# Two shifted copies inside SBUF: ScalarE's own copies against DMAs that ScalarE issues

## The reference

```python
pooled = x.mean(axis=(-2, -1))
gate = jax.nn.softmax(pooled @ gate_w.T + gate_b)
kw1 = jnp.einsum('be,eoihw->boihw', gate, experts_w1) + conv1_w      # kw2, kb1, kb2 likewise
out1 = jax.nn.relu(per_sample(x, kw1, kb1))                            # 3x3, SAME
out2 = per_sample(out1, kw2, kb2)                                      # 3x3, SAME
return identity + out2 * RES_SCALE
...
x = x + _L0_conv_ref(_gn(x), ...)
```

## Time and profile before

| | |
|---|---|
| median of 3 runs | 386.82 us (386.42, 386.82, 389.31) |
| span of the profiled execution | 389.2 us, first to last instruction |
| the profiled execution's own time | 389.31 us, the one of the three that holds the span |
| busy: PE, DVE, ACT, POOL | 84%, 79%, 77%, 11% of the span |
| mean granted TensorE clock | 0.940 of full speed |
| DMA traffic | 58.19 MB, mean 149 GB/s |

### The profile page before, as it was taken

The page is one execution under the profiler, slowest core; times in us unless marked ns, Lnnn a source line. Parts: engine busy times, 40 slices in busy tenths (PEclk is TensorE's granted clock), DMA queues, the critical chain, the costliest instruction groups (busy, mean ns, idle before and its releaser), DMA issues.

```text
span 389.2 us, 8418 instructions
## 1 busy us (share of the span) xinstructions
PE 326.8 (84%) x2983; PEld 198.4 (51%) x2983; DVE 308.1 (79%) x709; ACT 300.3 (77%) x373; POOL 44.5 (11%) x80
## 2 busy tenths in 40 slices
PE   3218698996999699996979979996999979999984
PEld 2117345654555355653535555653656545655663
DVE  4899978988689886998688797898689897777432
ACT  2357499986897968977897868978789768976950
POOL 7262302010100101010000101010010101000000
PEclk9556999998999989998999989999999989999998
DMA  7949915495948959396856949497885956092354
GB/s 169 224 95 196 205 30 125 107 203 137 202 92 187 182 142 220 86 210 148 178 127 149 223 111 203 96 196 147 188 167 123 217 128 147 22 207 53 92 123 121
DMA packets 107146, 58.19 MB, mean 149 GB/s; under 512 B 102496, under 2 KB 103008, under 8 KB 107104
## 3 DMA queue, kind: packets, MB, share of 16 engines
q1 hardware_dynamic: 106912, 57.62, 69.7%
q0 software_dynamic: 192, 0.01, 0.1%
HBM read 19.47 MB, written 18.87 MB: 99 GB/s over the span
## 4 chain that ended last, share of the span: by engine, by line
DVE 39%; PE 22%; issue 15%; ACT 13%; DMA 6%; SPq 3%; DVEq 1%; ACTq 0%
PE pg L393 20%; DVE mix L677 11%; DVE a L706 6%; DVE stats L621 6%; DVE img L718 5%; DMA c<-a 5%; ACT c L558 4%; ACT a L544 4%; ACT hid L544 2%; DVE a L668 2%; DVE wts L696 2%; DVE wts L699 2%; SPq L282 1%; DVE gate L661 1%; PE pg L357 1%
## 5 line engine op out<-in xcount | busy, mean ns | idle before, releaser
L393 PE MATMUL pg<-a,wts 128*64 128x480 f16 (+1 forms) x1440 | 303.5, 368 | 24.8 <-DVE img L718 18.2
L393 PE MATMUL pg<-c,wts 128*64 128x480 f16 (+1 forms) x1440 | 308.3, 372 | 6.1 <-ACT a L544 3.2
L393 PEld LDWEIGHTS pg<-c,wts 128*64 128x64 f16 x1440 | 156.1, 111 | 81.7 <-issue 6.8
L393 PEld LDWEIGHTS pg<-a,wts 128*64 128x64 f16 x1440 | 156.1, 112 | 64.5 <-issue 14.6
L544 ACT ACTIVATE hid<-pg,col 128x480 f32<-128x480 f32 (+3 forms) x112 | 58.9, 541 | 47.6 <-PE pg L393 25.6
L558 ACT COPY c<-a 64x2352 f32<-64x2352 f32 x32 | 68.7, 2148 | 0.2
L677 DVE SCALAR_TENSOR_TENSOR mix<-bank,gate,mix 128x386 f32<-128x386 f32 x96 | 63.9, 665 | 2.3
L706 DVE TENSOR_TENSOR a<-hid,a 128x480 f16<-128x480 f32 (+3 forms) x112 | 54.9, 512 | 12.2 <-ACT a L544 11.6
L544 ACT ACTIVATE a<-pg,col 128x480 f16<-128x480 f32 (+3 forms) x112 | 59.2, 544 | 0.4
L718 DVE SCALAR_TENSOR_TENSOR img<-pg,img 128x480 f32<-128x480 f32 (+1 forms) x80 | 48.1, 631 | 11.2 <-PE pg L393 9.9
L621 DVE BATCH_NORM_STATS2 stats<-img 128x6 f32<-128x384 f32 x96 | 45.5, 541 | 0.0
(11 more groups left out here) (60 smaller groups left out, 133.8 us busy)
## 6 DMA issues: line engine op xcount, KB each, us to landing
c<-a SPq DMA_DIRECT2D x28, 588.0 KB, 9.0
img<-in_x SPq DMA_DIRECT2D x56, 288.0 KB, 5.3
out<-img SPq DMA_DIRECT2D x60, 180.0 KB, 2.9
out<-img SPq DMA_DIRECT2D x60, 108.0 KB, 1.9
c<-a SPq DMA_DIRECT2D x8, 294.0 KB, 4.4
img<-in_x SPq DMA_DIRECT2D x16, 144.0 KB, 4.4
out<-img SPq DMA_DIRECT2D x4, 120.0 KB, 2.1
out<-img SPq DMA_DIRECT2D x8, 60.0 KB, 1.7
```

The lines of the kernel that those rows point to most:

```text
L393: last = nc.tensor.matmul(pg[g][side * 64:side * 64 + 64, at:at + nb * W].rearrange("p (b w) -> p b w", w=W), wts[s.c % WSETS][kind][:, v, ...
```

## The change

The two copies by ScalarE's datapath (L558, each of 64 partitions, seen as 32-bit words to halve their number) become two DMAs that ScalarE issues in the same place of its program. The waits ahead of them are the same. The DMAs read the same rows of `a2`, shifted by one block in one of the two halves, and write `c2`. TensorE's wait changes from one count by ScalarE to the landing of both DMAs (16 each), and the semaphore is split over a ring of six, so that the counts of two images are not mixed.

```diff
-        crossed2 = sem("crossed2")
+        crossed2 = [sem(f"crossed2_{i}") for i in range(RING)]
...
-                    pe.wait_ge(crossed2, s.number + 1)
+                    pe.wait_ge(crossed2[s.ring], 32 * (s.lap + 1))
...
-                d, a = (halves(k[t.parity])[half].rearrange("p a b w -> p a (b w)").bitcast(F32) for k in (c2, a2))
-                first = (1 - half) * RP // 2
-                last = nc.scalar.copy(d, a[:, :, first:first + NB * RP // 2])
-                if half == 1:
-                    last.then_inc(crossed2, 1)
+                first = 1 - half
+                act.dma_start(halves(c2[t.parity])[half][:, :, :, :].rearrange("p a b w -> p a (b w)"),
+                              halves(a2[t.parity])[half][:, :, first:first + NB, :].rearrange("p a b w -> p a (b w)")
+                              ).then_inc(crossed2[t.ring], 16)
```

## The result

The change costs 12%: **435.03 us** (4 runs, 432.43 to 437.19) against 387.23 (4 runs, 386.42 to 389.31), a ratio of 1.1203 with a 95% interval of 1.1132 to 1.1273. The forecast of 446 had the direction, the range and the size right, 59 us for a measured 48. Two of its reasons were not right, and the experiments show what stands in their place.

What follows compares the result with a forecast made beforehand. No engine has much room, so event order decides: PE would wait at conv2, 25.7 us a slot. Slots 2 to 15 add 52, slot 1 adds 5, slot 16 adds 2: 59 on 386.8 gives 446 us, range 408 to 492.

Steps and rivals of the forecast that it cites:

- The rhythm of before and its margin: Kernel before: 21.98 us a slot; `c2` ready 0.7 us early, 5.0 us from start of making to use.
- The size of the stall: PE at conv2 in each slot: waits for `c2` by L less 5.0, so 5.0 us.
- L: ScalarE's DMA pair for `c2`: time from first issue's start to the second DMA's landing, taken as 10.0 us.
- Slot 1: First slot's wait for `c2`: L about 9 in place of 4.3 us, costing 5 us.
- The clock: PE behind the stall at conv2: lower granted clock costs another 1.6 us a slot.
- The gap at the start of a slot goes away: PE ahead of conv1: no wait remains, since finish of group 0 is long done and VectorE has slack.
- the sharing of the engines: Two queues sharing DMA engines evenly: cross2's 6.0 us of transfer stretched by another 6.0, upper L 14.2.
- SP's stores start earlier and give time back to cross1: SP's queue: earlier stores give back some 3 us, so cross1 lands about 25.7 us into the slot, not 28.7.
- The DMA engines as the bound: Rival for every slot: L 14.2, slot 29.9 us, total 507, or 488 with cross1 as gate; chance 0.16.
- The faster side: Rival: pair lands within 5.0 us, PE doesn't wait, VectorE's lag sets the slot; 361 to 374 us, chance 0.04.
- ScalarE's freed time: Copies leaving ScalarE: 2.2 to 3.1 us a slot stay free, gain counted as nothing if PE waits at conv2.

Runs made afterwards that it cites:

- The filler: Changed kernel plus five unneeded fp32 matmuls ahead of TensorE's wait for `c2` in every slot: 443.58 us, runs from 427.52 to 449.63.
- the reorder: Changed kernel with cross1 issued ahead of the loads in SP's order from slot 2 on: 414.41 us, 1.060; the same edit in the kernel before: 0.991.
- the kernel with idle DMAs: Kernel before, keeping ScalarE's copies, plus the change's two DMAs in the same place into a tile that nobody reads: 427.22 us, ratio 1.094.
- the twelfth-size kernel: Changed kernel with each `c2` DMA moving 2 of 24 block rows, the rest of `c2` set to zero once: 377.16 us, ratio 0.967.

## Why the prediction was right, and where its steps were not

**The rhythm of before and its margin** held: 5.0 us from start to use, cross1 as the gate of every other slot. PE waits for `c2` in each slot, as forecast.

**The size of the stall** was off, 5.0 us forecast and 2.7 in most slots. L was taken as 10.0 and is 8.7 in slot 4: that is 1.3 us. ScalarE issues 1.1 us ahead of the place where its copies began, which I had as a bound only: that is the rest. In slots 3 and 11, where the pair took 11.7 and 11.4 us, the stall was over 5.

**Slot 1** was to cost 5 us and cost 1.5. L is 9.3 there, as forecast (about 9), but the pair goes out at 52.15, 3.2 us ahead of the copies of before (55.38 in the earlier trace rows).

**The clock** was as forecast, 1.7 us, in 11 of the 13 slots from 2 to 14. The length of the wait alone does not decide it: over the four microseconds behind a wait of 2.38 us in slot 13 the granted clock is 0.66, behind 1.89 us in slot 10 and 2.41 us in slot 14 it is 1.00, and so it is behind 3.44 us in slot 4 of the changed kernel with cross1 first. The filler shows that its cost is partly hidden behind cross1.

**"The gap at the start of a slot goes away"** failed ahead of three slots, with 2.4 to 2.8 us each. Two of these gaps are cross1's; the third, 2.42 us ahead of slot 8, ends on nothing that the profile names. Ahead of six others cross1 landed 0.6 us or less before PE began. The step that failed is the sharing of the engines: I stretched cross2 by the other queue's traffic, up to 14.2. In most slots it is SP's issues that are stretched, the loads' by 5 us in slot 4, and cross2 comes through almost undisturbed. That SP's stores start earlier and give time back to cross1 was right: they start 2.3 us ahead of slot 4, where they started 2.3 us into slot 10 before. So the two changes nearly cancel: cross1 lands 23.6 us into the slot, where 25.7 was forecast and 22.7 was read before. The shorter slot leaves it no margin all the same.

Added up from slot 2 to slot 15, a slot has on average 3.0 us of stall where 5.0 was forecast, 0.6 us of gaps at its start where none was, and 20.9 us of convolutions with the clock's loss where 20.7 was (rounded): 24.56 us for the forecast 25.7. By the traces, 33.5 of their 41.4 us lie in slots 2 to 14, 6.4 behind the start of slot 15, 1.5 ahead of slot 2. That the total came so near owes something to luck: the stall was too long and the gap missing. The forecast's mechanism, a PE that waits at conv2 in each slot, is only one of two that bind together: with cross1's part taken away by the reorder the loss is half as large, and without the wait, as the kernel with idle DMAs shows, 9.4% would have remained.

**The rivals.** The DMA engines as the bound (0.16) had more truth in it than its chance. It probably holds once `c2` and cross1 are both in time (1.023), not in the changed kernel, whose DMA engines are busy 0.90 of the time. The faster side (0.04) fails at its point: L was never under 5.0 with full-sized DMAs, the shortest was 7.9. Where it was, in the twelfth-size kernel, the time did fall, by 14 us and not 26, since cross1 still gated. ScalarE's freed time was forecast as worth nothing while PE waits. No run tests that alone; in the trace ScalarE's waits for PE grow from 25.6 to 99.5 us, more than the 68.7 us of its copies.

The Trainium skill's page "DMA: Bandwidth & Descriptors" (Issuing engines are not separate DMA queues) says that DMAs of different engines run on the same 16 DMA engines and interleave. The runs agree: 49 KB took 8.7 us instead of 2.2 behind another queue's pair. That they are shared evenly, which I added for the upper L, the trace does not bear out: 7.9 to 9.3 in fourteen of sixteen pairs and 11.7 at most, not 14.2.

## What to carry to other kernels

Here a DMA that takes the place of a copy is paid twice: in the wait of whoever needs it, and in every transfer that shares the engines with it, so look first for the latest transfer on which something already waits, here cross1. Idle DMAs into a tile that nobody reads price that second part in one run, and a fraction of the bytes prices what freeing the engine is worth. When two waits bind together, taking one away gives back only what the other lets through.

## What the runs showed of the hardware

- DMAs issued while a pair of 588 KB ones was under way took longer to issue, whichever queue the pair was on: four loads of 288 KB took 7.91 us beside ScalarE's pair and 8.33 us behind SP's own pair, against 2.95. A pair issued just behind the loads was stretched itself, to 11.7 us against 8.2 alone. That the loads have rows of 384 bytes and the pair rows of 4704 may play a part; no run varied it.
- ScalarE's sequencer issues a DMA before the activations ahead of it in program order have run: at 128.94, when the first of `hidden(s, 1)` starts, the second following at 129.49.
- An issue on one queue can itself be held while the other queue issues: 3.62 us for two on ScalarE with SP's stores starting at 121.05, and nothing computed behind it for 2.74 us. This was seen in two of sixteen pairs.
- GpSimd copies 64x2352 words in 2140 ns, ScalarE in 2150.
